# New orders in front of both choices of experts and of the attention's projections, in a macaron block on one Trainium2 core

## The reference

```python
x = x + 0.5 * ffn(layernorm(x))      # 32 experts, the best 8 of a token, 128 slots each
x = x + attn(layernorm(x))           # 16 heads of 8, a low-rank K/V of 128, a shared rope part of 32
x = x + 0.5 * ffn(layernorm(x))      # the same weights
# ffn: logits = x @ gate.T; softmax; top_k(8); weights normalised over the 8
#      pos = running count of earlier tokens of the same expert; beyond 128 slots dropped
#      h = silu(buf @ gate) * (buf @ up); out = weighted sum of h @ down
# attn: c = x @ W_kv_down; k, v from c; q from x; rope parts from c and x
#      causal softmax((q.k + qr.kr) / sqrt(40)); heads joined; @ W_o
```

## Time and profile before

| | |
|---|---|
| median of 3 runs | 555.93 us (555.92 to 560.0) |
| the profiled execution | 558.29 us, its span 556.6 us |
| TensorE busy, mean granted clock | 516.7 us (93%), 0.971 |
| VectorE, ScalarE, GpSimd busy | 419.8, 256.1, 97.6 us |
| chain that ended last | PE 76%, DVE 9%, DMA 4%, POOL 3% |

### The profile page before, as it was taken

How to read it: one execution, slowest core, us unless ns; L and a number is a source line. 1 busy time by engine, 2 the same in 40 slices (tenths; PEclk the granted TensorE clock), 3 DMA queues, 4 the chain that set the end, 5 groups by cost and what they waited for, 6 DMA issues and landing times.

```text
span 556.6 us, 11051 instructions
## 1 busy us (share of the span) xinstructions
PE 516.7 (93%) x3522; PEld 330.3 (59%) x3522; DVE 419.8 (75%) x1425; ACT 256.1 (46%) x429; POOL 97.6 (18%) x215
## 2 busy tenths in 40 slices
PE   5979999987899899999999999999999786999995
PEld 2856777863356455555555555655545553676774
DVE  4885989874789687777778777778713968898874
ACT  1844222244533456665665556566577621222222
POOL 2210000011593113031221303121223110000000
PEclk8989999997999899999999999999999969999999
DMA  8895200000044001010100001010000340000002
GB/s 187 171 268 163 48 1 3 1 2 2 0 153 181 29 24 36 5 52 4 39 22 28 30 13 46 2 47 14 0 2 1 118 138 2 1 2 2 1 3 75
DMA packets 25094, 26.70 MB, mean 48 GB/s; under 512 B 6704, under 2 KB 18576, under 8 KB 25040
## 3 DMA queue, kind: packets, MB, share of 16 engines
q1 hardware_dynamic: 24176, 25.63, 16.1%
q10 hardware_dynamic: 864, 0.36, 0.2%
HBM read 17.04 MB, written 8.78 MB: 46 GB/s over the span
## 4 chain that ended last, share of the span: by engine, by line
PE 76%; DVE 9%; DMA 4%; POOL 3%; SPq 2%; ACT 2%; issue 2%; DVEq 0%; ACTq 0%
PE ps L1638 13%; PE ps L1727 13%; PE ps L1664 12%; PE ps L1343 10%; PE ps L1429 7%; PE ps L1444 5%; PE ps L1460 3%; DVE xn L850 2%; PE ps L1634 2%; PE ps L1334 2%; PE ps L1693 2%; DMA x<-in_L_attn_x 1%; PE ps L1257 1%; DMA kn_d<-nl 1%; DVE stats L826 1%
## 5 line engine op out<-in xcount | busy, mean ns | idle before, releaser
L760 ACT ACTIVATE probs<-ps 128x1024 f32<-128x1024 f32 (+3 forms) x192 | 145.9, 811 | 97.1 <-PE ps L1664 96.9
L1178 DVE TENSOR_REDUCE mxh<-ps 128x1 f32<-128x512 f32 (+2 forms) x176 | 114.8, 686 | 28.7 <-PE ps L1638 28.1
L1638 PE MATMUL ps<-Kst,Qst 120*128 120x512 f32 (+3 forms) x384 | 129.2, 402 | 3.5 <-DMA Qst<-qn_d 2.2
L1664 PE MATMUL ps<-Qst,Kst 121*128 121x512 f32 (+3 forms) x384 | 94.4, 352 | 1.2 <-ACT probs L760 0.7
L1638 PEld LDWEIGHTS ps<-Kst,Qst 120*128 120x128 f32 x384 | 66.2, 191 | 45.8 <-DVE mxh L1178 17.2
L514 POOL TENSOR_SCALAR_AFFINE_SELECT probs<-probs 128x256 f32<-128x256 f32 x128 | 51.4, 406 | 200.0 <-ACT probs L760 198.7
L1175 DVE CUSTOM_DVE_ANT_0 summed<-ps,maskf 128x384 f32<-128x384 f32 (+1 forms) x128 | 74.3, 618 | 13.5 <-PE ps L1638 13.5
L1727 PE MATMUL ps<-probs,Vst 128*32 128x512 f32 (+3 forms) x768 | 81.8, 499 | 0.1
L1664 PEld LDWEIGHTS ps<-Qst,Kst 121*128 121x128 f32 x384 | 67.0, 190 | 15.5 <-ACT probs L760 5.7
L1343 PE MATMUL ps<-onehot,xp 128*128 128x512 bf16 (+1 forms) x264 | 68.8, 385 | 7.7 <-DVE onehot L929 6.9
L929 DVE TENSOR_SCALAR onehot<-iotab,posm 128x128 bf16<-128x128 bf16 (+1 forms) x352 | 60.4, 250 | 0.2
(11 more groups left out here) (180 smaller groups left out, 614.9 us busy)
## 6 DMA issues: line engine op xcount, KB each, us to landing
wgn<-in_L_ffn_gate_up_proj SPq DMA_DIRECT2D x8, 384.0 KB, 5.2
guT_d<-gus SPq DMA_DIRECT2D x6, 384.0 KB, 2.7
gus<-guT_d SPq DMA_DIRECT2D x6, 384.0 KB, 5.9
Kst<-kn_d SPq DMA_DIRECT2D x28, 64.0 KB
Qst<-qn_d SPq DMA_DIRECT2D x28, 64.0 KB
wdn<-in_L_ffn_down_proj SPq DMA_DIRECT2D x8, 192.0 KB, 6.2
dnT_d<-dns SPq DMA_DIRECT2D x6, 192.0 KB, 3.6
dns<-dnT_d SPq DMA_DIRECT2D x6, 192.0 KB, 7.7
```

The costliest lines, as they stand in the source:

```text
L760: e.activation(probs[n % RING][:, 2 * b:2 * b + 2, lo:BANK], ps[:, 2 * b:2 * b + 2, lo:BANK], ACT.Exp, scale=SCALE).then_inc(probs_ready, 1)
L1178: e.tensor_reduce(to, s.rearrange("p (q k) -> p q k", k=w), AX.X, ALU.max).then_inc(mx_ready, 1)
L1638: ins = e.matmul(ps[:, bank, i * w:(i + 1) * w], Qst[p][h][0:ROWS, column(b, jt * P):column(b, jt * P) + P], Kst[p][h][0:ROWS, column(b, o ...
L1664: ins = e.matmul(ps[:, 2 * b + h, lo:BANK], Kst[p][h][0:ROWS + 1, column(b, kt * P):column(b, kt * P) + P], Qst[p][h][0:ROWS + 1, column(b ...
```

## The change

No instruction that computes anything is added or removed, apart from matmuls on zeros. Calls change place:

- **First choice.** ScalarE's load of the exponential's table moves from behind the first copy of logits to a place behind the fourth. The weight sets 0 to 4 are copied later (`copy_weights(4)` before `experts(0)`), and TensorE turns set 1 behind `positions(0, 0)` and set 4 behind `positions(0, 3)`, followed by five idle matmuls.
- **`close`.** The first two sums are turned before the third and the fourth are finished, and the last `combine` no longer waits for half of `eol` before it closes its first banks. In the first round the root's table is loaded between the copies.
- **Projections' front.** Roots stand between ScalarE's copies, idle matmuls between TensorE's turns, the rope of `x` before the wait for `ckvT`.
- **Stores.** `store_nope` of pieces 4 to 7 is issued by ScalarE's queue, two behind each of the first two copies of `V`.
- **Second choice.** Twelve idle matmuls in front of the last turn instead of two, one less behind the logits, none around the first two `positions`, four and eight later.

```diff
             def step(c, p, h=0, first=False, last=False):
                     if first and k == 0:
-                        copy_weights(5)
                         copy_weights(6)
...
                     e.activation(yT[:, j * BANK:(j + 1) * BANK], ps[:, 4 + j, :], ACT.Copy).then_inc(yT_ready, 1)
+                    if k == 0 and i == 1:
+                        table_for(ACT.Sqrt)
...
             copy_logits(0, 0)
-            table_for(ACT.Exp)
             first_part(0, 1)
-            copy_weights(0)
             turned_out(0, 2)
             copy_logits(0, 1)
             second_part(0, 0)
             first_part(0, 2)
             turned_out(0, 3)
             copy_logits(0, 2)
+            copy_weights(0)
             first_part(0, 3)
             second_part(0, 1)
+            copy_logits(0, 3)
             copy_weights(1)
-            copy_logits(0, 3)
             second_part(0, 2)
+            table_for(ACT.Exp)
             copy_weights(2)
             second_part(0, 3)
             copy_weights(3)
             exps(0)
+            copy_weights(4)
             experts(0)
...
-            for g in range(NG):
-                root(1, g)
+            root(1, 0)
+            root(1, 1)
             e.wait_ge(w_stored, 32 * (NCH - RING))
...
-            transposed(1, after=compressed)
+            turned_out(1, 0)
+            root(1, 2)
+            compressed(0)
+            root(1, 3)
+            turned_out(1, 1)
+            compressed(1)
+            turned_out(1, 2)
+            turned_out(1, 3)
+            compressed(2)
+            compressed(3)
             table_for(ACT.Exp)
...
                 e.activation(V[:, TG * g:TG * (g + 1), :, :].rearrange("p a b c -> p (a b c)"), ps[:, g, :], ACT.Copy).then_inc(v_ready, 1)
+                if g < RING:
+                    store_nope(e, NC + 2 * g)
+                    store_nope(e, NC + 2 * g + 1)
...
                     for j in (2, 3):
                         e.matmul(ps[:, 4 + j, :], zerosb[:, 0:P], zerosb[:, :], start=False, stop=True, skip_group_check=True).then_inc(y_closed, 1)
+                    turn_sums(0)
...
-                    turn_sums(0)
+                    turn_sums(1)
...
-                    e.wait_ge(eol_ready, 2 * (u + 1) + 1)
+                    if c < NCH - 1:
+                        e.wait_ge(eol_ready, 2 * (u + 1) + 1)
...
             e.wait_ge(xnT_ready, 2 * NG + RING)
-            e.wait_ge(ckvT_ready, NC)
             rope(0)
             low(0)
+            e.wait_ge(ckvT_ready, NC)
             low(1)
...
-            turn(3, 3, xn, 2)
+            turn(3, 3, xn, 12)
             logits(1, 2, 2)
-            logits(1, 3, 2)
-            idle_work(0, 2)
+            logits(1, 3, 1)
             positions(1, 0)
-            idle_work(0, 2)
             positions(1, 1)
             idle_work(0, 2)
             positions(1, 2)
-            idle_work(0, 2)
+            idle_work(0, 4)
             positions(1, 3)
+            idle_work(0, 8)
             experts(1)
```

More of the change, by code:

```diff
@@ L1268, in turn @@
                 ins.then_inc(turned, 1)
-            def transposes(n, src, after=None):
-                for g in range(NG):
-                    turn(n, g, src)
-                    if after and g >= 1:
-                        after(g - 1)
-                if after:
-                    after(NG - 1)
             def logits(k, i, idle=1):
@@ L1498, in _ @@
             positions(0, 0)
+            turn_weights(1)
             positions(0, 1)
```

52 lines of the change are left out of this document (28 added, 24 removed).

## The result

| | us |
| --- | --- |
| before | 556.55, median of 4 runs (555.92 to 560.0) |
| changed | 550.19, median of 4 runs (548.38 to 550.67) |
| ratio | 0.988, 95% interval 0.985 to 0.992 |
| profiled execution of the changed kernel | 550.67, its span 549.0 |

The change makes the kernel 6.4 us faster. The forecast was 12.9 us and 543.0, the range 540 to 549: the prediction was wrong. The sign was right, and so were two of the four parts of its sum, the two choices of experts. To see which, I cut the two profiled executions at five instructions: the last down matmuls of the first experts, the first matmul of the rope, the exponentials of step 7 of pair 0, the first one-hot of the second choice, and the last add.

What follows compares the result with a forecast made beforehand. It took the chain that ended last, 76% TensorE, as the bound. Terms -0.4 - 5.0 - 3.5 - 4.0 = -12.9 us took the profiled 558.29 to 545.4, and the median 555.93 to 543.0; range 540.0 to 549.0.

Steps and rivals of the forecast that it cites:

- First choice: First choice of experts: later table load delays the places, a full-clock gather gives it back; -0.4 us, net -0.9 to -0.1.
- Adds: Sums ahead of the projections: first add 1.15 us sooner, VectorE 1.5 us ahead to its last tile, 130.6 instead of 132.12.
- Projections' front: Sums to rope: sooner adds, reordered copies and full TensorE clock bring the rope from 138.41 to 133.45, -5.0 us.
- A compress is half of 2.08/2: Projections' front: the duration of one compress at full clock, used in the walk from the turns to the rope.
- the rival with idle matmuls at half the clock: Idle matmuls take 0.43 us each ahead of real work; rope at 142.7, kernel slower at 562.7; chance 0.03.
- Stores: Start of attention: ScalarE issues second stores sooner, second staging ends 2.7 us sooner, TensorE's stall and half clock go; -3.5 us.
- at the 4.2 us that it takes now from there to the staging: Start of attention: last store's issue to second staging still takes 4.2 us, so staging starts at about 177.
- The stores land no sooner: Start of attention: all queues share 16 DMA engines, so earlier issue gains nothing; 546.3 us, chance 0.09.
- Second choice: Second choice of experts: idle matmuls keep TensorE's clock full, logits 1.5 us sooner, 2.50 us wait goes; -4.0 us.
- the full clock up to 460: Second choice: expected sign that TensorE's clock stays at 1.00 from 440 to 460 us.
- End: End of the kernel: last sum starts 0.4 us later, second add's wait goes; 0 us, between +0.4 and -0.7.

Runs made afterwards that it cites:

- p_first: Kernel before with only the first choice's edits (table load and weight copies moved, one turn out of the first expert step, five idle matmuls): 558.35 us, ratio 1.001.
- a_none: Changed kernel without the 17 idle matmuls between turns and compresses in the projections' front, the sixteen ahead kept: 549.74 us, ratio 0.986.
- b_layout: Kernel before with kn_d and qn_d laid out head by head, all stores still issued by SP: 556.4 us, ratio 0.998.
- a_layout: Changed kernel with kn_d and qn_d laid out head by head, so 64 KB staging DMAs read 16 neighbouring rows: 546.05 us, ratio 0.976.
- a_layout_sp: Changed kernel with the head-by-head layout and the second stores issued by SP again: 546.44 us, ratio 0.982.
- a_again: The changed kernel run once more, unaltered, on the chip of the other three: 550.17 us, ratio 0.985 to the kernel before.
- a_split: Changed kernel, its layout kept, each 64 KB staging DMA issued as two of 8 rows: 544.91 us, ratio 0.978.

## Why the prediction was wrong, step by step

- **First choice**, -0.4: measured 0.5 to 0.6 faster at equal clock. Its mechanism is right (late table, late places, quick gather), and its size as far as a scatter of 0.6 lets one tell. What the sum left out is that the moment at which the clock rises in the front differs between executions by up to 8.5 us (14.0 to 22.5), at some 0.4 us each: 3.4 us, about half of the spread of the runs (555.1 to 562.4 in nineteen of the kernel before). The other half isn't traced. This scatter may be why p_first alone shows nothing in its time.
- **Adds**: the first add 1.15 us sooner and VectorE's last tile 1.5; measured 1.24 and 1.75 (18.44 to 16.69 us behind the last down matmuls). Right.
- **Projections' front**, -5.0: measured -3.7. The step that failed is "A compress is half of 2.08/2". One compress is the whole row, both of its matmul records, 2.08 us at half clock: 1.12 us at full clock, not 0.52. I read `x2` as two compresses. Two of them stand in the chain ahead of turn 1 and turn 2, and two behind turn 3. With the right size my own walk would have shown that the sixteen and the seventeen idle matmuls stood in front of work that was ready. The last tile was ready at 131.68, its turn came at 133.68. The clock stayed up, as forecast, but the idle matmuls were not needed for it (a_none). The same misreading stands in the rival with idle matmuls at half the clock: by its own prices its sum gives 144.5 and not 142.7, and 148.6 with 2.08 for a compress. It did not occur.
- **Stores**, -3.5: measured +0.4. This is the step that decided. The issues came a little sooner than forecast (the last by 3.4 us); what failed is "at the 4.2 us that it takes now from there to the staging". In the kernel before, and wherever the staging is wide, the step does take that: 4.23 us (b_layout), 4.33 (a_layout, 170.43 to 174.76), 4.36 (a_layout_sp). But the forecast carried it over to a time in which the first staging was still in the DMA engines. Before, that staging ran from 167 to 172 at a share of 0.24 and the stores behind it. In the changed kernel both ran together and filled the engines until 172, and a tail was left that two of sixteen DMA engines work off at 53 GB/s: four DMAs of 64 KB are 262 KB, 4.9 us. The last store, issued 3.4 us sooner, took 8.01 us to the staging (169.62 to 177.63).

  In all ten profiled executions with narrow staging the second staging starts 13.7 to 14.6 us behind the first, whoever issues the stores. That fits a sum of work on two engines that no order of issues changes; by the rule above I estimate for each of them 131 KB of staging, 131 KB of the eight stores and 16 KB of the 32 KB stagings, 10.5 us at 26.5 GB/s. It is argued, as no row shows a single engine. And the start of the second staging was not the whole lever either: b_layout lost its wait with a start only 0.5 us sooner, because the staging itself got quicker.

  The rival "The stores land no sooner", at 0.09, is what happened (its time should read 543.0 + 3.5 = 546.5). Its argument, that the DMA engines have work before the last store and that work stays, was the right one, though the 4.2 us that it leaned on are no sign of it; the Trainium skill's rule, in DMA: Bandwidth & Descriptors, section Issuing engines are not separate DMA queues, agrees. I priced it low because SP's queue held the stores until 170.62, and didn't look at what the DMA engines did in the time into which they would move.
- **Second choice**, -4.0: measured -4.7 in the stretch, -4.2 alone. Right, to the wait of 2.50 us that goes. Only the full clock up to 460 failed (0.50 from 455 to 457), at no price that the stretches show.
- **End**, 0 between +0.4 and -0.7: -0.4 to -0.6. Inside.

The terms as measured at equal clock: -0.6 - 3.7 + 0.4 - 4.4 - 0.5 = -8.8. The times say -6.4 in the first comparison; in the second the medians say -7.7 (557.85 to 550.17) and the ratio, 0.9845, -8.6. Of the 7.2 us between the forecast, 543.0, and the measured 550.2, the stores bring 3.9 and the mis-read compress 1.3, while the other terms give back 1.1. Another 0.6 is the median before, which a fourth run moved from 555.93 to 556.55. The last 2.5 us fit the clock of the front: all four timed executions of the changed kernel show a mean clock of 0.984, as the profiled one does, in which the clock was up at 21.0; a_again's profiled one, up at 15.5, has 0.988. That is argued from the mean, not seen in each execution.

## What to carry to other kernels

Before moving a DMA to another queue, look at what the DMA engines do in the gap that you want to close: a busy share near 2/16 with a low rate was the sign of narrow transfers here, and those were mended by their shape (16 rows outermost, or more DMAs), not by their issuer. Look there too at the time into which the DMA would move: a time from issue to landing holds only beside the same neighbours. Ask of an `xN` row how many instructions of the program it is before a duration is divided. And compare two executions stretch by stretch at the same state of TensorE's clock, or a microsecond of luck in the front hides one that was earned.

## What the runs showed of the hardware

- Four DMAs from [2, 8, 1024] to 16 rows, with stores of 256 KB beside them, left a tail of five microseconds at 0.14 of the DMA engines and 53 to 55 GB/s (changed); the same bytes as 16 rows (a_layout), or as twice 8 rows (a_split), leave no such tail.
- A store of 256 KB took 4.2 to 4.4 us from its issue to the staging that waited for it where no narrow staging ran beside it, and 8.0 where one did.
- The same program has TensorE's full clock in its front from 15.5 us on or from 21.0 us on.
- TensorE kept 1.00 through gaps of 0.75 and 0.69 us between short pieces of work (a_none), and went to 0.50 behind one of 2.64 us (changed). Behind one of 2.0 us it went to 0.50 in one execution and stayed at 1.00 in another of the same program (changed, a_again).
- A table load of 1.28 us stands in ScalarE's queue and nothing more: the next activation starts 0.01 us behind it (28.80 + 1.28 to 30.09). Put between two copies of `yT` (118.22), it delays nothing: the copy behind it ends at 120.2, and its turn stands in TensorE's queue until 121.51.
